# Selective stage of a four-layer transformer on one core: filter input's base, update of x and W2's bias on GpSimd, average over heads behind the spectrum

## The reference, cut to what matters

```
Q = x_text @ Wq;  K = x_vision @ Wk                    # 4 heads of 32, 120 context rows
scores = Q K / sqrt(32), masked by vision_mask
attn = softmax over the 32 highest scores of each token, 0 elsewhere
attn_mean = attn.mean over heads                       # "average over heads"
c_t = (attn_mean @ (x_vision @ Wv)) * text_mask
x = layernorm(x_text, g_norm_in, b_norm_in)
scale_in, shift_in = split(c_t @ W_film_in + b_film_in)
x = x * (1 + gate * scale_in) + gate * shift_in        # the filter's input u
y = s4d(x)                                             # long filter: rfft, product, irfft, + x * D_skip
scale_out, shift_out = split(c_t @ W_film_out + b_film_out)
y = y * (1 + gate * scale_out) + gate * shift_out
xt = x_text + y
h = gelu(layernorm(xt, g_ffn, b_ffn) @ W1 + b1) @ W2 + b2
return layernorm(xt + h, g_norm_out, b_norm_out)       # added to the residual x
```

## Time and profile before

| what | us |
|---|---|
| median of 3 runs | 4385.09 |
| lowest and highest run | 4382.11, 4387.93 |
| the profiled execution's own time | 4379.5 |
| its span, first to last instruction | 4377.6 |
| selective stage in the span, about | 3509 to 4150 |

### The profile page before, as it was taken

The page is one execution under the profiler, slowest core; times in us unless marked ns, Lnnn a source line. Parts: engine busy times, 40 slices in busy tenths (PEclk is TensorE's granted clock), DMA queues, the critical chain, the costliest instruction groups (busy, mean ns, idle before and its releaser), DMA issues. The chain is left out here.

```text
span 4377.6 us, 70189 instructions
## 1 busy us (share of the span) xinstructions
PE 4028.9 (92%) x23076; PEld 3180.3 (73%) x23076; DVE 3217.2 (73%) x7695; ACT 2280.8 (52%) x5400; POOL 570.5 (13%) x1096
## 2 busy tenths in 40 slices
PE   7997997999779999999999999999999779999788
PEld 5886775777558788777777877777787547667565
DVE  6995666676767777777777777767777579999457
ACT  3554664555445556555655655656556134444344
POOL 1331001101230000000000000000033323333211
PEclk9998998999889999999999999999999679999899
DMA  3001000000000000000000000000000200000001
GB/s 98 0 0 39 0 0 1 0 0 0 15 7 1 2 4 2 5 1 2 4 2 5 1 3 4 2 5 1 2 2 10 57 10 1 0 0 0 16 27 39
DMA packets 34256, 40.44 MB, mean 9 GB/s; under 512 B 6272, under 2 KB 30475, under 8 KB 33935
## 3 DMA queue, kind: packets, MB, share of 16 engines
q1 hardware_dynamic: 33200, 36.90, 2.9%
q10 hardware_dynamic: 800, 0.33, 0.0%
HBM read 32.77 MB, written 4.19 MB: 8 GB/s over the span
## 5 line engine op out<-in xcount | busy, mean ns | idle before, releaser
L1724 ACT ACTIVATE global_prob_t_high<-psum 128x512 fp32r<-128x512 f32 x960 | 569.8, 601 | 585.9 <-PE psum L1838 585.9
L1632 DVE TENSOR_TENSOR global_prob_t_low<-psum,global_prob_t_high 128x512 fp32r<-128x512 f32 x960 | 656.6, 689 | 250.9 <-ACT global_prob_t_high L1724 236.9
L1638 DVE TENSOR_REDUCE global_top<-psum 128x1 f32<-128x480 f32 x1024 | 666.0, 657 | 108.3 <-PE psum L1798 103.1
L1796 PE MATMUL psum<-global_prob_t_high,global_v_low 128*128 128x512 f32 x960 | 456.1, 475 | 0.9
L1796 PE MATMUL psum<-global_k_high,global_q_low 128*128 128x480 f32 x1024 | 390.7, 382 | 14.3 <-ACT spare L1745 12.0
L1798 PE MATMUL psum<-global_k_high,global_q_high 128*128 128x480 f32 x1024 | 391.9, 383 | 0.0
L1797 PE MATMUL psum<-global_k_low,global_q_high 128*128 128x480 f32 x1024 | 388.6, 380 | 0.0
L1797 PE MATMUL psum<-global_prob_t_low,global_v_high 128*128 128x512 f32 x960 | 379.8, 396 | 0.0
L1798 PE MATMUL psum<-global_prob_t_high,global_v_high 128*128 128x512 f32 x960 | 379.5, 395 | 0.0
L1745 ACT ACTIVATE spare<-psum,global_bias 128x480 f32<-128x480 f32 x512 | 337.1, 663 | 16.5 <-DVE global_bias L1641 15.1
L1745 ACT ACTIVATE global_prob<-psum,global_bias 128x480 f32<-128x480 f32 x512 | 337.2, 662 | 1.3
(11 more groups left out here) (471 smaller groups left out, 8354.5 us busy)
## 6 DMA issues: line engine op xcount, KB each, us to landing
x_res<-in_x SPq DMA_DIRECT2D x8, 512.0 KB, 9.6
moe_we<-in_expert_t SPq DMA_DIRECT2D x8, 512.0 KB, 7.5
out<-x_res SPq DMA_DIRECT2D x16, 256.0 KB, 2.1
cho_wqkv<-in_L_ffn_Wqkv SPq DMA_DIRECT2D x2, 1536.0 KB
self_ctx_t<-in_ctx_t SPq DMA_DIRECT2D x2, 1440.0 KB, 13.6
sel_w<-in_L_xattn_W SPq DMA_DIRECT2D x2, 1024.0 KB, 10.8
global_ctx_t<-in_ctx_t SPq DMA_DIRECT2D x1, 1440.0 KB
sel_ctx_t<-in_ctx_t SPq DMA_DIRECT2D x1, 1440.0 KB
```

The lines of the kernel that those rows point to most:

```text
L1632: dve.tensor_tensor(dst, psum, high.bitcast(F32), ALU.subtract).then_inc(ready.sem, 1)
L1638: ins = dve.tensor_reduce(top[:, c:c + 1], w.psum[:, c, 0:chunk], AX.X, ALU.max)
L1724: act.activation(dst, psum, ACT.Copy).then_inc(ready.sem, 1)
L1796: pe.matmul(to, lhs_low, rhs_high, start=start, stop=False)
```

## The change

Eight edits in one stage; what is computed stays the same.

1. The base of the filter's input (T) leaves DVE: ACT makes xl times 1/sigma behind the copy of Q (two 128x256 activations), POOL multiplies by g_norm_in and adds b_norm_in. 1/sigma (`rstd_normed`) no longer waits on POOL for `u_base`.
2. The update of x (done) leaves DVE: POOL multiplies y by g_norm_out, adds b_norm_out and adds to x. POOL's earlier addition of b_norm_out to x (L2386) goes; ACT's y now waits for `x_updated` of the batch before.
3. W2's bias is no longer a matmul. POOL makes `xt_biased` = xt + b2 and DVE adds W2's product to it. b2 is loaded to all partitions (128 KB) instead of to two. The four preparing DVE operations go.
4. W2's product goes to PSUM banks 6 and 7. The forward transform no longer waits for `ffn_kept`; the backward transform, which writes banks 6 and 7, does. The last two quarters of W1 stand in those banks, so W2 waits for all Gelus (`hid_ready` 3) instead of the first two quarters.
5. `average` is split: `weigh` stays behind the choice; the average over heads runs one iteration later, for F, on DVE behind the spectrum and the statistics of M.
6. The transposes of the average on PE move from before the forward transform to behind the scores (PSUM bank 2), and their copy on ACT moves behind the copy of Q and the base.
7. The first half of the context product now stands between those transposes and the FiLM product in, where it stood behind the FiLM product before.
8. On DVE the statistics of M stand behind the spectrum instead of before it.

```
-    rows_high = sb("rows_high", [2, D], F32R)
-    row_parts = sb("row_parts", [P, D], F32R)
-    is_low = sb("is_low", [2, 1])
-    ones_r = sb("ones_r", [P, P], F32R)
+    xt_biased = sb("xt_biased", [P, LANES, D])
...
                     i, p = M
                     need(pool, "xl_ready", i - 1)
                     scale_rows(pool, chain, "a", i)
-                    need(pool, "u_base", i - 2)
                     scale_normed_rows(pool, chain, p)
                 if now:
                     i, p = now
                     scale_rows(pool, chain, "b", 2 * i)
-                    need(pool, "xl_ready", i)
-                    pool.tensor_tensor(both_tiles(i), both_tiles(i),
-                                       rows["b_norm_out"][:, :].unsqueeze(1).to_broadcast([P, LANES, D]),
-                                       ALU.add).then_inc(sig("x_biased").sem, 1)
+                    need(pool, "xt_made", i)
+                    need(pool, "ffn_kept", i - 1)
+                    pool.tensor_tensor(xt_biased[:, :, :], xt, of_both("b2"), ALU.add).then_inc(sig("xt_kept").sem, 1)
                 if F:
                     i, p = F
-                    need(pool, "u_base", i)
                     need(pool, "film_in_ready", i)
                     chain.link(pool.tensor_tensor(u_in[p], u_in[p], mods_in[:, :, 0:D], ALU.mult))
                     pool.tensor_tensor(u_in[p], u_in[p], mods_in[:, :, D:2 * D],
                                        ALU.add).then_inc(sig("u_ready").sem, 1)
+                if T:
+                    i, p = T
+                    need(pool, "u_base", i)
+                    chain.link(pool.tensor_tensor(u_in[p], u_in[p], of_both("g_norm_in"), ALU.mult))
+                    chain.link(pool.tensor_tensor(u_in[p], u_in[p], of_both("b_norm_in"), ALU.add))
+                if done is not None:
+                    need(pool, "yn_ready", done)
+                    chain.link(pool.tensor_tensor(y, y, of_both("g_norm_out"), ALU.mult))
+                    chain.link(pool.tensor_tensor(y, y, of_both("b_norm_out"), ALU.add))
+                    pool.tensor_tensor(both_tiles(done), both_tiles(done), y, ALU.add).then_inc(sig("x_updated").sem, 1)
+                if F:
+                    i, p = F
                     need(pool, "film_out_ready", i)
                     need(pool, "xt_made", i - 2)
                     pool.tensor_tensor(xt_base[p], xl[p], shift_out, ALU.add).then_inc(sig("base_ready").sem, 1)
...
-            def prepare_bias():
-                dve.tensor_scalar(is_low[:, :], w.ident[0:2, 1:2], -1.0, None, ALU.mult)
-                dve.tensor_copy(ones_r[:, :], w.ones[:, :])
-                dve.memset(row_parts[:, :].bitcast(F32), 0.0)
-                link(dve.tensor_copy(rows_high[:, :], bias_rows[:, :]))
-                dve.scalar_tensor_tensor(row_parts[0:2, :], rows_high[:, :].bitcast(F32), is_low[:, :],
-                                         bias_rows[:, :], ALU.mult, ALU.add).then_inc(rows_ready.sem, 1)
-
+            def add_skip():
...
-            def average(i):
+            def weigh(i):
...
+
+            def average(i):
                 need(dve, "mean_t_psum", i - 1)
...
                 if done is not None:
                     need(dve, "ffn_psum", done)
-                    link(dve.tensor_tensor(xt, w.psum[:, 4:6, 0:D], xt, ALU.add))
+                    need(dve, "xt_kept", done)
+                    link(dve.tensor_tensor(xt, w.psum[:, 6:8, 0:D], xt_biased[:, :, :], ALU.add))
                     dve.engine_nop().then_inc(sig("ffn_kept").sem, 1)
                     stats("b", 2 * done + 1, lambda s: xt[:, s, :])
-                if M:
-                    i, p = M
-                    need(dve, "rstd_normed", i - 1)
-                    stats("a", i, x_tile(i))
...
-                if T:
-                    i, p = T
-                    need(dve, "freq_psum", 2 * (i - 2) + 1)
-                    need(dve, "xl_ready", i)
-                    need(dve, "rstd_normed", i)
-                    for s in range(LANES):
-                        ins = dve.scalar_tensor_tensor(u_in[p][:, s, :], xl[p][:, s, :], rstd_of_normed[p][:, s:s + 1],
-                                                       rows["g_norm_in"][:, :], ALU.mult, ALU.mult)
-                    link(ins)
-                    dve.tensor_tensor(u_in[p], u_in[p], rows["b_norm_in"][:, :].unsqueeze(1).to_broadcast([P, LANES, D]),
-                                      ALU.add).then_inc(sig("u_base").sem, 1)
-                if done is not None:
-                    need(dve, "yn_ready", done)
-                    link(dve.tensor_tensor(y, y, rows["g_norm_out"][:, :].unsqueeze(1).to_broadcast([P, LANES, D]),
-                                           ALU.mult))
-                    need(dve, "x_biased", done)
-                    dve.tensor_tensor(both_tiles(done), both_tiles(done), y, ALU.add).then_inc(sig("x_updated").sem, 1)
+                if M:
+                    i, p = M
+                    need(dve, "rstd_normed", i - 1)
+                    stats("a", i, x_tile(i))
+                if F:
+                    average(F[0])
                 if now:
                     i, p = now
...
                     choose(i)
-                    average(i)
+                    weigh(i)
                 if T and isinstance(T[0], int) and T[0] == 0:
-                    prepare_bias()
+                    add_skip()
...
-                if F:
-                    i, p = F
-                    need(act, "mean_t_psum", i)
-                    act.activation(mean_t[0:NCTX, :, :], w.psum[0:NCTX, 1, 0:LANES * P].rearrange(
-                        "p (l t) -> p l t", t=P), ACT.Copy).then_inc(sig("mean_t_ready").sem, 1)
                 if done is not None:
                     need(act, "rstd_b", 2 * done + 1)
+                    need(act, "x_updated", done - 1)
                     normalise("b", lambda s: xt[:, s, :], y).then_inc(sig("yn_ready").sem, 1)
...
+                    need(act, "rstd_normed", i)
+                    need(act, "freq_psum", 2 * (i - 2) + 1)
+                    for s in range(LANES):
+                        ins = act.activation(u_in[p][:, s, :], xl[p][:, s, :], ACT.Copy,
+                                             scale=rstd_of_normed[p][:, s:s + 1])
+                    ins.then_inc(sig("u_base").sem, 1)
+                if F:
+                    i, p = F
+                    need(act, "mean_t_psum", i)
+                    act.activation(mean_t[0:NCTX, :, :], w.psum[0:NCTX, 2, 0:LANES * P].rearrange(
+                        "p (l t) -> p l t", t=P), ACT.Copy).then_inc(sig("mean_t_ready").sem, 1)
...
-                if F:
-                    i, p = F
-                    need(pe, "mean_ready", i)
-                    for s in range(LANES):
-                        last = pe.transpose(w.psum[0:NCTX, 1, s * P:(s + 1) * P], mean[:, s, :], w.ident[:, :])
-                    last.then_inc(sig("mean_t_psum").sem, 1)
...
-                    need(pe, "ffn_kept", i - 1)
...
-                if F:
-                    need(pe, "mean_t_ready", F[0])
...
+                    need(pe, "ffn_kept", i - 1)
...
+                if T and isinstance(T[0], int) and T[0] == 0:
+                    values_by_film()
                 if F:
                     i, p = F
                     need(pe, "film_out_ready", i - 1)
+                    need(pe, "mean_ready", i)
+                    for s in range(LANES):
+                        last = pe.transpose(w.psum[0:NCTX, 2, s * P:(s + 1) * P], mean[:, s, :], w.ident[:, :])
+                    last.then_inc(sig("mean_t_psum").sem, 1)
+                if T:
+                    ctx_by_film(T[0], 0)
+                if F:
+                    i, p = F
+                    need(pe, "mean_t_ready", i)
                     need(pe, "ctx_film_ready", 2 * i + 1)
                     films(i, p, "film_in")
-                if T and isinstance(T[0], int) and T[0] == 0:
-                    values_by_film()
-                if T:
-                    ctx_by_film(T[0], 0)
...
-                    need(pe, "hid_ready", i * 4 + 1)
-                    if isinstance(i, int) and i == 0:
-                        pe.wait_ge(rows_ready.sem, rows_ready.count(0))
-                    for s in range(LANES):
-                        pe.matmul(w.psum[:, 4 + s, 0:D], ones_r[:, :], row_parts[:, :], start=True, stop=False)
+                    need(pe, "hid_ready", i * 4 + 3)
                     for j in range(HT):
-                        if j % 2 == 0 and j >= 4:
-                            need(pe, "hid_ready", i * 4 + j // 2)
                         for s in range(LANES):
-                            last = pe.matmul(w.psum[:, 4 + s, 0:D], hid[:, j, s, :], w2[:, j, :],
-                                             start=False, stop=(j == HT - 1))
+                            last = pe.matmul(w.psum[:, 6 + s, 0:D], hid[:, j, s, :], w2[:, j, :],
```

(1 more changed line is left out.)

15 lines of the change are left out of this document (8 added, 7 removed).

## The result

| kernel | runs | median us | lowest and highest |
|---|---|---|---|
| before | 15 | 4383.97 | 4379.81, 4387.93 |
| changed | 15 | 4395.72 | 4387.56, 4402.10 |

The ratio is 1.0026 [1.0019, 1.0034]: 11.75 us slower. The forecast was 4402, its range 4383 to 4419, its sign slower; what was named as most likely is what the trace shows, with sizes that differ. The profiled execution of the changed kernel has a span of 4396.3 us and a time of 4398.1.

What follows compares the result with a forecast made beforehand. DVE bounds the kernel before, PE the changed one. Iterations +4.0, fill -3, drain -1.9 and end +2.5 give +1.6 us; clock falls add +15.5: 4379.5 becomes 4396.6, 4402 on the runs' scale, range 4383 to 4419.

Steps and rivals of the forecast that it cites:

- The bound: In the changed stage's iterations PE becomes the bound, at 35.58 us against 31.97 for DVE.
- the stall: On PE before the transposes of h, behind the FiLM product in: a wait of 2.42 us where it was 0.70.
- The walk: PE's steps added through one iteration of the new order: 35.58 us against 35.27, +4.0 for thirteen iterations.
- DVE's room: In front of W2's end and the spectrum, DVE was to have 3.6 us of new idle time per iteration.
- The clock: PE's granted clock falls after the wait before h in 9 of 14 iterations, 1.72 us each: +15.5 us.
- case 2: Rival, chance 0.24: PE waits before h but the clock holds; +1.6 us, 4387, counted as the same.
- The fill: At the stage's start, the base of two batches leaves DVE where PE waits for it: -3 us.
- The drain and the end: Two draining iterations lose waits of 0.93 on DVE, -1.9; POOL's update of x at the stage's end adds +2.5.
- POOL's new work is safe beside the choice: POOL's large operations beside DVE's choice keep their usual 1.27 us, so moved work there was taken as safe.
- The last rival: Chance 0.16: POOL holds DVE in the average and its statistics; over its 0.5 us margin PE waits too, 4418.
- DVE sets the pace: In the kernel before, DVE is one closed chain with almost no wait; PE follows it, less than 2 us behind.
- Case 3: Rival, chance 0.12: faster, 4357; DVE remains the bound and the wait before h is not on the path.

Runs made afterwards that it cites:

- experiment 4: Edits 1 and 2 alone on the kernel before: 4408.46 us; with POOL's base and update waiting for DVE's small operation: 4387.44; that wait in the changed kernel: 4397.90.

## Why the prediction was right, and where its steps were off

**The bound, and the stall: right.** The wait before the transposes of h was worked out as 2.42 us and is 2.42 in every iteration. The walk gave 35.58 us; the periods without a fall are 35.43 to 35.48. The step from the FiLM product to h was put at 4.41 and is 4.30 (3741.58 to 3745.88), which is most of the difference. DVE's room was put at 3.6 us, in front of W2's end and the spectrum. In an iteration without a fall it is 1.83 before W2's end and 0.41 and 0.44 in the spectrum; the small operation that POOL holds takes 0.76 of the rest, and the weights (L2464, 1.65 us instead of 1.16) another 0.49. `xt_base` was to have some 10 us of room and has 4.07: the kernel before has 10.30, and the five new operations come out of that. Against 35.27 the schedule costs 13 x 0.18 = 2.4 us, not 4.0.

**The clock: right in kind, slightly small.** The forecast had 9 of 14 iterations at 1.72 us, 15.5. Nine of thirteen fell in the profiled execution, and a tenth in the iteration ahead of the first W2, which the table counts in the start of the stage; 475.11 less 13 x 35.455 is 14.2 us, 1.58 each. The granted clock behind the wait is 0.62 over 4 us where 0.57 was taken: (1 - 0.62) x 4 = 1.52. Filling the stall gave back 14.9 us between medians (4396.21 - 4381.35), and 13 in the profiled iterations, which is more than the whole slowdown. The reading of the earlier trace rows behind it, that 1.60 holds and 1.97 can fall, stood: 1.56 held, and seven of ten waits of 1.91 to 2.14 fell. Why only nine of thirteen fall, for one and the same wait, is not explained. The forecast's nine of fourteen was guessed between its two bounds; that it comes so close is luck. In the four profiled executions with this wait, two to four long periods stand between two short ones.

Waits of 2.42 us in a loop that is otherwise full were enough for a fall, as was a pair of 1.17 and 0.49, so case 2, in which the clock holds (chance 0.24), is out. The rule of the Trainium skill that the clock falls only at longer gaps (TensorE: Matmul & The Clock Gate, HAM oscillation) is not borne out by these rows.

**The ends: mis-sized.** The fill was put at -3 and is -6.06. The estimate took only the base off DVE's path. But PE stood in front of the transposes of the average for 4.31 and 6.52 us in the fill of the kernel before. The new order has these behind the scores, where they wait for nothing. The first wait is gone with that (from the second K of T to the third it takes 5.2 us less); the second comes back as one of 5.69 for DVE in front of the forward transform. PE before, then after:

```profile
3548.26 0.68 PE L2710 MATMUL psum<-ident,sel_mean 128*120 128x128 f32 x2 [4.31 <-DVEq L2479]
3578.05 0.68 PE L2710 MATMUL psum<-ident,sel_mean 128*120 128x128 f32 x2 [6.52 <-DVEq L2479]
```
```profile
3581.05 5.25 PE L2709 MATMUL psum<-powers,sel_forward 128*128 128x256 f32 x16 [5.69 <-DVE sel_w L2432]
```

The drain and the end were put at -1.9 and +2.5, together +0.6; they are -0.87. From the last W2 on it is +2.7 (17.17 us before, 19.87 after), near the forecast, so the drain is -3.6. The three operations of POOL are there and end 3.9 us after the first starts, close to the 4.0.

**The sum.** The forecast's +17.1 on its own scale stands against 9.7 in the stage and 11.75 between the medians. The fill's 3, the schedule's 1.6, the clock's 1.3 and the end's 1.5 account for 7.4 of it. All four erred to the same side, so nothing cancelled. The forecast also began from a median of 4385.1, which is 4384.0 with more runs. These are the known parts of the way from 4402 to 4395.7; stage and medians themselves differ by 2 us.

**Contention: the step "POOL's new work is safe beside the choice" was wrong.** It read POOL's durations, which did keep 1.27, and not DVE's. One DVE operation inside the choice is held for 0.7 to 1.1 us (0.84 to 1.27 instead of 0.17). With the moves alone the new work holds it; in the changed kernel it is an old operation of u, which the new order has brought beside it, and `xt_base` lengthens the weights in four of thirteen iterations. In the changed kernel this falls into idle time; experiment 4 shows it to be 21 us, with the clock, where DVE's loop is closed. The last rival's place, the average, was not where it happened: the average's six products take 1.86 us together, 1.87 before. Its margin, put at 0.5 us, is 0.8.

**"DVE sets the pace" needs a finer reading.** It is true that the loop through DVE was closed and had no slack, but shortening DVE by 3.12 us alone gave nothing (experiment 4, 0.26 us in thirteen iterations), since the time reappears as a wait for the backward transform. The loop ran through both engines. Only the new order of PE, with the average and the bias out of its way, made the period shorter, 34.6 and then 33.9 instead of 35.3, and this the changed kernel hid behind one stall. Case 3 had that gain (4357) with a chance of 0.12 and ACT's fixed order against it; putting the context product back under ACT's two steps was the way to it, at 4369 and 4362.

**The spread.** The changed kernel's fifteen runs lie 14.5 us apart, those of the kernel before 8.1. A number of falls that varies from run to run would do this, at 1.6 us each; only a profiled execution shows single falls, so this is argued, not shown. Each run's mean granted clock over the whole program goes with it, 0.961 in the three runs of 4390.6 to 4391.6 us and 0.958 to 0.959 in the four from 4398.1 up, but it varies with the time in the kernel before as well (0.961 to 0.964).

## What to carry to other kernels

Before moving work off the engine that looks like the bound, follow its loop: if its next operation waits for another engine that waits for it, the time comes back as a wait. When reordering TensorE, ask of each pair of neighbours whether a third engine must work between them, and keep a product there to cover it; a wait of 2.4 us in each iteration cost 1.1 us by the clock, and by the schedule 0.2 against the kernel before and 0.9 against the order that covers it (34.6 us). Put GpSimd's long operations where no short VectorE operation of a closed loop meets them, and read VectorE's rows for it, not GpSimd's.

## What the runs showed of the hardware

- TensorE's clock dropped from 2.4 to 1.2 GHz behind waits of 2.42 us inside a loop in which it is otherwise busy, in 9 or 10 of 13 iterations, and behind 7 of 10 waits of 1.91 to 2.14; that cost 1.4 to 1.6 us each time. It stayed behind thirteen single waits of 1.56 us and behind single ones of 1.60 and 1.69. Pairs of 1.16 to 1.18 and 0.49 to 1.05 us with 0.43 us of work between them dropped it in 7 of 10, while pairs of 0.46 and 1.05 never did. Two waits of some 2.3 and 2.42 in nearly each iteration held the mean at 0.89.
- Idle TensorE time filled with one matmul of a size that is needed anyway (0.86 us, computed twice) kept the clock at 1.00 and took 13 us off both the median and the thirteen iterations.
- A VectorE `TENSOR_SCALAR` of 128x8 took 0.84 to 1.27 us instead of 0.17 beside a GpSimd operation of 128x512, and ended 0.01 to 0.04 us behind it. A `SCALAR_TENSOR_TENSOR` of 128x960 took 1.65 to 1.75 instead of 1.16. MAX8 and MATCH_REPLACE8 were not held.
- Two activations of 128x256 with a scale for each row take 0.90 us together on ScalarE, which had been estimated at 1.0.
